# Key pairs laid out by ScalarE, multiplied in two GpSimd instructions and folded from 16 to 8

## The chip, the cores and the metric

One Trainium2 chip, the kernel on one of its cores. The metric is the device time of one execution in microseconds (us). A core has five engines that run their own instruction streams and wait for each other by semaphores: TensorE (PE; its weight loads are PEld), VectorE (DVE), ScalarE (ACT), GpSimd (POOL) and SyncE (SP), which here issues the DMAs.

## What is computed

A model of six stages over 32 images of 256 tokens with 192 features. The change is in the third, an attention with a choice of key pairs, which runs on two halves (t) of 128 tokens of each image, for 12 heads of 16 features. For each token i and head the 8 most similar earlier keys are found; then every set {i, a} (8 of them) and {i, a, b} (28) is scored by the log of the determinant of its Gram matrix, and the output is a mean of the sets' values, weighted by the softmax of the scores:

```python
_, top_idx = jax.lax.top_k(sim, M)                      # M = 8
...
K = k[idx]; V = v[idx]                                  # i, and one or two of the 8
gram = jnp.einsum('cnd,cmd->cnm', K, K)
det = jnp.linalg.det(gram)
log_det = jnp.log(jnp.where(valid, det, 1.0) + 1e-06)
score = SIGN * log_det / float(s + 1) ** ALPHA
dot = jnp.einsum('cnd,d->cn', K, q_i) / HS ** 0.5
w = jax.nn.softmax(dot, axis=1)
out_s = jnp.einsum('cn,cnd->cd', w, V)
...
probs = jax.nn.softmax(scores / TEMP)
y_soft = probs @ outs
```

The off-diagonal Gram entries are 36 dot products of 16 elements for each token and head: 8 of a gathered key with the token's own key, 28 of two gathered keys. The change is in how these 36 are made.

## The kernel before

The attention phase is `dpp_attention_phase`. An image is worked on in 12 steps; a step handles two heads (j = 0, 1) of one half of 128 tokens; steps 0 to 5 are the near half t = 0 (128 keys), steps 6 to 11 the far half t = 1 (256 keys). Every engine runs the same loop of bodies, body i of image n, two images in one turn of a hardware loop, and in body i it does its part of step i and of earlier steps, with fixed lags that the code writes out:

- VectorE, body i: `max` and `max_index` (L2530, L2537) find the 8 best keys of step i; L2545 makes the one-hot matrices of step i-2 (one instruction for a near step, two for a far one, 2048 bf16 elements each); L2554 sums the products of step i-4 into `dots`; then comes one stage of the previous image's scoring (bodies 0, 1, 3 to 7), the value sum `y` (L2513, bodies 8 and 9), or in body 11 the residual (L2520) and the next image's own norms (L2379, L2380).
- ScalarE, body i: casts the found indices of step i (`cast_index`, L2205); copies what TensorE gathered of step i-3, head pair j = 0, out of PSUM (`take_gathered`: keys L2222, values L2223, norms L2224, then `kv_ready`); copies the turned indices (`copy_turned`, L2213) that SyncE then sends out and back as a broadcast; the same for j = 1; then the stage's activation (such as the logarithm of the denominators, L2241), the copies of the next image's projections (L2175 to L2188) and others.
- TensorE, body i: scores of step i+1, the gather of step i-3, j = 0 (L2679; 24 small matmuls in a near step, 48 in a far one), the turn of step i's indices (L2660), the gather of j = 1, then a part of the next image's projections.
- GpSimd, body i: `products` of step i-3, and then in bodies 7 and 8 `weigh` (L2323: values times weights, 1728 elements, one for each half), in body 10 `squares`, in body 11 `split_rest`, in body 0 `split_low`.

So the products of a step that GpSimd makes in body i are summed by VectorE in body i+1. Before the change GpSimd makes them in eight instructions: for each j three over broadcast views of the eight keys (4, 4 and 16 pairs of 16 elements: 64, 64 and 256 elements a partition; L2334), and then for both j together the four remaining pairs (L2339) and the eight with the token's own key (L2340). It can begin on j = 0 while j = 1 is still on its way, and its result has the rows `prod[P, parity, j, 36, 16]`, which L2554 sums over the last axis. The buffers have two parities of step. ScalarE waits for `prod_ready` of two steps earlier before it overwrites `keys`; GpSimd waits for `dots_ready` of two steps earlier before it overwrites `prod`.

Keys, values and products are fp32; the one-hot matrices and the pieces that are gathered with them are bf16.

## Time and profile before

| what | value |
|---|---|
| runs of the kernel before | 6936.29 us (median of 3, 6931.03 to 6949.35) |
| the profiled execution, its own time | 6937.07 us |
| its span on the core | 6935.4 us |
| busy in the span | PE 5118.2, PEld 3716.5, DVE 4327.0, ACT 2100.8, POOL 3276.0 us |
| mean granted TensorE clock | 0.718 |
| `dots` sums (L2554) | 384, 517.0 us, mean 1346 ns |
| products, pairs (L2334) | 2304, mean 514 ns, 1115.6 us |
| products with the own key (L2340) | 384, mean 835 ns, 320.7 us |
| copies of keys (L2222) | 768, mean 264 ns, 202.5 us |

A group's busy time counts each instruction from its start to its end; on ScalarE consecutive instructions overlap, so that the sum of their lengths is more than the time they take. The idle time of an engine is put down to the one whose semaphore came last. The page's chain of the work that ended last covers the end of the last stage of the model only and says nothing of the attention phase, which lies between about 1595 and 4450 us of the span.

### The profile page before, as it was taken

The page shows a single profiled execution, that of the slowest core. Times are in us where ns is not written, and L with a number is a line of the kernel's source. Part 1 is how long each engine was busy: PE and PEld are TensorE (multiplying, and loading weights), DVE is VectorE, ACT ScalarE, POOL GpSimd, SP SyncE. Part 2 cuts the span into 40 slices and gives each one's busy share as a digit, 9 for nine tenths or more (in the row PEclk, how much of TensorE's full clock was granted, in tenths as well). Part 3 has the DMA queues.
Part 4 walks back from the last instruction along what each step waited for, and adds up shares of the span by engine and source line. Part 5 has one row for each costly group of instructions (what it writes and reads, how often), then busy time and mean ns, then how long its engine had stood idle before and what let it go on. Part 6 is the DMA issues. An engine that isn't in the chain of part 4 may idle for free. (4 is left out here: it accounts for less than half of the span.)

```text
span 6935.4 us, 140450 instructions
## 1 busy us (share of the span) xinstructions
PE 5118.2 (74%) x45364; PEld 3716.5 (54%) x45365; DVE 4327.0 (62%) x9002; ACT 2100.8 (30%) x6098; POOL 3276.0 (47%) x4341
## 2 busy tenths in 40 slices
PE   6776766978888888888888888443980997169990
PEld 2333333765555555556555665342860776169990
DVE  5777775227888898898999999722654233212223
ACT  3343333223333333333333333222210332223330
POOL 1222222115666776777776767425236000554447
PEclk8677776996666666666666666556995997579995
DMA  4000000002222222222222222202222002111113
GB/s 138 5 7 5 7 3 6 0 5 71 74 74 70 75 72 72 73 75 71 74 72 72 75 72 75 67 26 73 75 72 68 0 0 60 52 50 46 46 42 109
DMA packets 170739, 369.46 MB, mean 53 GB/s; under 512 B 35650, under 2 KB 100939, under 8 KB 169140
## 3 DMA queue, kind: packets, MB, share of 16 engines
q1 hardware_dynamic: 136404, 283.77, 12.2%
q0 software_dynamic: 33792, 78.69, 3.6%
q8 instruction: 312, 5.11, 0.3%
q14 instruction: 231, 1.89, 0.1%
HBM read 286.86 MB, written 75.50 MB: 52 GB/s over the span
## 5 line engine op out<-in xcount | busy, mean ns | idle before, releaser
L2334 POOL TENSOR_TENSOR l2a_prod<-l2a_keys 128x64 f32<-128x64 f32 (+1 forms) x2304 | 1115.6, 514 | 817.2 <-ACT l2a_norms L2224 808.2
L2679 PE MATMUL l2a_g<-l2a_feat,l2a_onehot 128*128 128x33 bf16 x27648 | 894.1, 187 | 29.9 <-issue 24.8
L2679 PEld LDWEIGHTS l2a_g<-l2a_feat,l2a_onehot 128*128 128x128 bf16 x27648 | 835.8, 103 | 89.5 <-issue 61.1
L2648 PE MATMUL l2a_s<-l2a_qkT 32*128 32x128 f32 (+1 forms) x1536 | 653.6, 518 | 48.3 <-issue 48.3
L1734 POOL TENSOR_TENSOR l_hc<-l_hs,l_bc 128x512 f32<-128x512 f32 x192 | 243.0, 1266 | 803.2 <-DVE l_hs L1808 799.7
L2554 DVE TENSOR_REDUCE l2a_dots<-l2a_prod 128x72 f32<-128x1152 f32 x384 | 517.0, 1346 | 154.3 <-POOL l2a_prod L2340 154.3
L2545 DVE TENSOR_SCALAR l2a_onehot<-l2a_spread,l2a_key_col 128x2048 bf16<-128x2048 bf16 x576 | 544.7, 972 | 52.0 <-PE l2a_g L2679 45.0
L1903 PE MATMUL l_y<-l_hc,l_selT 128*96 128x512 f32 x384 | 316.5, 920 | 287.9 <-POOL l_hc L1734 287.9
L2597 PE MATMUL l2a_a<-l2a_tT,l2a_wqk 96*96 96x256 f32 x1024 | 453.4, 622 | 0.7 <-ACT l2a_tT L2175 0.7
L2648 PEld LDWEIGHTS l2a_s<-l2a_qkT 32*128 32x128 f32 x1536 | 320.5, 259 | 224.6 <-issue 181.7
L440 POOL DMA_INDIRECT rows_in<-l3f_dispatch_xn,l3f_dispatch_at x128 | 122.8, 959 | 651.2 <-ACT l3f_dispatch_xn L416 612.5
L2222 ACT COPY l2a_keys<-l2a_g 128x128 f32<-128x128 f32 x768 | 202.5, 264 | 687.5 <-PE l2a_g L2679 687.1
L652 POOL TENSOR_TENSOR l3f_w_own<-l3f_w,l3f_w_own 96x1536 fp32r<-96x1536 f32 x72 | 252.5, 3507 | 329.7 <-DVE l3f_w_own L753 329.7
L2660 PE MATMUL l2a_t<-l2a_ident_bf,l2a_index 128*16 128x128 bf16 x384 | 101.2, 264 | 368.1 <-ACT l2a_index L2205 367.8
L695 PE MATMUL l3f_expert_h<-l3f_tT,l3f_w_own 96*128 96x256 f32 x2592 | 337.1, 289 | 8.9 <-POOL l3f_w_own L652 6.7
L695 PEld LDWEIGHTS l3f_expert_h<-l3f_tT,l3f_w_own 96*128 96x128 f32 x2592 | 323.8, 193 | 9.6 <-issue 7.1
L2340 POOL TENSOR_TENSOR l2a_prod<-l2a_keys,l2a_feat 128x256 f32<-128x256 f32 x384 | 320.7, 835 | 0.0
L2597 PEld LDWEIGHTS l2a_a<-l2a_tT,l2a_wqk 96*96 96x96 f32 x1024 | 261.9, 270 | 108.0 <-ACT l2a_tT L2175 1.1
L759 DVE TENSOR_TENSOR l3f_tT<-l3f_expert_tp,l3f_tT 96x512 fp32r<-96x512 f32 x72 | 49.5, 687 | 425.3 <-ACT l3f_tT L726 425.3
L735 ACT ACTIVATE l3f_hT<-l3f_expert_h,l3f_b 128x256 f32<-128x256 f32 x432 | 181.0, 470 | 383.6 <-PE l3f_expert_h L695 383.6
L710 PE MATMUL l3f_expert_y<-l3f_w,l3f_hT 128*128 x1728 | 292.6, 326 | 0.0
L1808 DVE TENSOR_TENSOR_SCAN l_hs<-l_dA,l_state,l_dBu 128x512 f32<-128x512 f32 x192 | 262.3, 1366 | 40.0 <-ACT l_dA L1684 33.7
(403 smaller groups left out, 11255.9 us busy)
## 6 DMA issues: line engine op xcount, KB each, us to landing
l2a_spread<-index_rows SPq DMA_DIRECT2D x384, 512.0 KB
rows_in<-main_zeros SPq DMA_DIRECT2D x1, 13824.0 KB, 59.4
l2f_xg<-rows_in SPq DMA_DIRECT2D x72, 192.0 KB, 2.4
rows_out<-l2f_ys POOLq DMA_DIRECT2D x72, 192.0 KB, 2.4
l3f_xg<-rows_in SPq DMA_DIRECT2D x72, 192.0 KB, 2.4
rows_out<-l3f_ys POOLq DMA_DIRECT2D x72, 192.0 KB, 2.4
l3f_w<-in_l3f_w SPq DMA_DIRECT2D x2, 4608.0 KB, 33.6
l_xT<-in_l_xT SPq DMA_DIRECT2D x16, 384.0 KB, 3.9
```

Of the source, the lines that this page charges most:

```text
L652: nc.gpsimd.tensor_tensor(w1_own[:, u, 1, :, :], w1[:, :, bass.ds(e, 1), :].rearrange("p h a f -> p h (a f)"), w1_own[:, u, 0, :, :].bitca ...
L695: ins = nc.tensor.matmul(h_ps[b][:, c % 2, :], w1_own[:, u, wp, h, c * P:(c + 1) * P], tT[:, u, tp_, h, :], start=h == 0 and wp == tp_, st ...
L710: ins = nc.tensor.matmul(y_ps[u][:, t * C:(t + 1) * C], hT[:, u, c, t * P:(t + 1) * P], w2[:, c, bass.ds(e, 1), :].rearrange("p a c -> p ( ...
L1808: nc.vector.tensor_tensor_scan(hs[:, g % 2, :], dA[:, g % 2, :], dBu[:, g % 2, :], state[:, 0, g:g + 1], ALU.mult, ALU.add).then_inc(scan_ ...
L1903: nc.tensor.matmul(y_ps[:, :], selT[:, g, :], hc[:, g % 2, :], start=g == 0, stop=g == G - 1).then_inc(hc_used, 1)
L2334: nc.gpsimd.tensor_tensor(made[:, j, at:at + wide * wide, :].rearrange("p (b a) f -> p b a f", b=wide), key[:, lo:lo + wide, :].unsqueeze( ...
L2340: nc.gpsimd.tensor_tensor(made[:, :, 0:8, :], both, feat[:, u, t, h:h + 4:3, 0:HS].unsqueeze(2).broadcast_to([P, 2, SLOTS, HS]), ALU.mult) ...
L2545: ins = nc.vector.tensor_scalar(onehot[:, s[2] % 2, kt, :, :].rearrange("p k t -> p (k t)"), spread[:, s[2] % 2, :, :].rearrange("p k t -> ...
L2554: nc.vector.tensor_reduce(dots[:, h:h + 4:3, :], prod[:, s[2] % 2, :, :, :], AX.X, ALU.add).then_inc(S["dots_ready"], 1)
L2597: ins = nc.tensor.matmul(o[0:HC, j * T:(j + 1) * T], wqk[:, h, 2 * (k - 1) + j, :], tT[0:HC, h, :], start=h == 0, stop=h == 1)
L2648: nc.tensor.matmul(o, qkT[rows, u, h // 3, t * P:(t + 1) * P], qkT[rows, u, 4 + h // 3, 0:nk], start=True, stop=False, skip_group_check=True)
L2679: ins = nc.tensor.matmul(g_ps[j][:, a * FEAT:(a + 1) * FEAT], onehot[:, s[2] % 2, kt, j * SLOTS + a, :], feat3[:, s[1], kt, piece, h, :], ...
```

## The change

ScalarE now writes the keys of a step not once but as two lists of operands. `left` (36 rows of 16) has the eight keys in rows 0 to 7 and then the 28 first keys of the pairs, `right` (28 rows) the 28 second keys, with the broadcasts done in the copies: seven copies in place of one, 1024 elements in place of 128, for each j, all read from PSUM. GpSimd multiplies `left` by `right` in one instruction for both j (2 x 448 elements), multiplies the first eight rows by the token's own key in a second (256 elements; the same operands as before but in place), waits for its own semaphore `products`, and adds the second eight elements of every row to the first (72 rows, 576 elements). VectorE sums over 8 elements in place of 16. `right` and `left` take the place of `keys` and `prod`. GpSimd waits for both j before it begins, and no longer for `dots_ready`; ScalarE waits for `dots_ready` of two steps earlier in place of `prod_ready`.

```diff
-        keys = m.sb("keys", [P, 2, 2, SLOTS, HS])
+        left = m.sb("left", [P, 2, 2, NCOMB, HS])
+        right = m.sb("right", [P, 2, 2, COMBS, HS])
...
-        prod = m.sb("prod", [P, 2, 2, NCOMB, HS])
...
                     if j == 0:
-                        act.wait_ge(S["prod_ready"], counted(q - 1) if not (isinstance(q, int) and q < 2) else 1)
+                        act.wait_ge(S["dots_ready"], counted(q - 1) if not (isinstance(q, int) and q < 2) else 1)
...
-                    nc.scalar.copy(keys[:, s[2] % 2, j, :, :], src[:, :, 0:HS])
+                    key, lo, hi = src[:, :, 0:HS], left[:, s[2] % 2, j, :, :], right[:, s[2] % 2, j, :, :]
+                    halves = key.rearrange("p (g k) f -> p g k f", g=2)
+                    nc.scalar.copy(lo[:, 0:SLOTS, :], key)
+                    nc.scalar.copy(lo[:, 8:12, :], key[:, 0:8:2, :])
+                    nc.scalar.copy(hi[:, 0:4, :], key[:, 1:8:2, :])
+                    nc.scalar.copy(lo[:, 12:20, :].rearrange("p (g b a) f -> p g b a f", g=2, b=2),
+                                   halves[:, :, 0:2, :].unsqueeze(2).broadcast_to([P, 2, 2, 2, HS]))
+                    nc.scalar.copy(hi[:, 4:12, :].rearrange("p (g b a) f -> p g b a f", g=2, b=2),
+                                   halves[:, :, 2:4, :].unsqueeze(3).broadcast_to([P, 2, 2, 2, HS]))
+                    nc.scalar.copy(lo[:, 20:36, :].rearrange("p (b a) f -> p b a f", b=4),
+                                   key[:, 0:4, :].unsqueeze(1).broadcast_to([P, 4, 4, HS]))
+                    nc.scalar.copy(hi[:, 12:28, :].rearrange("p (b a) f -> p b a f", b=4),
+                                   key[:, 4:8, :].unsqueeze(2).broadcast_to([P, 4, 4, HS]))
...
-                    pool.wait_ge(S["dots_ready"], counted(q - 1) if not (isinstance(q, int) and q < 2) else 1)
-                    made, h = prod[:, s[2] % 2, :, :, :], first_head(s[2])
-                    for j in range(2):
-                        pool.wait_ge(S["kv_ready"], counted(q * 2 + (j + 1)))
...
+                    made, h = left[:, s[2] % 2, :, :, :], first_head(s[2])
+                    pool.wait_ge(S["kv_ready"], counted(q * 2 + 2))
+                    hi = right[:, s[2] % 2, :, :, :]
+                    nc.gpsimd.tensor_tensor(made[:, :, SLOTS:, :].rearrange("p j k f -> p j (k f)"),
+                                            made[:, :, SLOTS:, :].rearrange("p j k f -> p j (k f)"),
+                                            hi.rearrange("p j k f -> p j (k f)"), ALU.mult)
+                    ins = nc.gpsimd.tensor_tensor(
+                        made[:, :, 0:SLOTS, :], made[:, :, 0:SLOTS, :],
+                        feat[:, u, t, h:h + 4:3, 0:HS].unsqueeze(2).broadcast_to([P, 2, SLOTS, HS]), ALU.mult)
+                    ins.then_inc(S["products"], 1)
+                    pool.wait_ge(S["products"], q + 1)
+                    every = made.rearrange("p j k f -> p (j k) f")
+                    nc.gpsimd.tensor_tensor(every[:, :, 0:HS // 2], every[:, :, 0:HS // 2], every[:, :, HS // 2:],
+                                            ALU.add).then_inc(S["prod_ready"], 1)
...
-                        nc.vector.tensor_reduce(dots[:, h:h + 4:3, :], prod[:, s[2] % 2, :, :, :], AX.X, ALU.add
+                        nc.vector.tensor_reduce(dots[:, h:h + 4:3, :], left[:, s[2] % 2, :, :, 0:HS // 2], AX.X, ALU.add
```

ScalarE's order, from the cast of a body's indices to the end of the second take, before:

```order
L2205 CAST l2a_index<-l2a_found 128x16
L2222 COPY l2a_keys<-l2a_g 128x128
L2223 COPY l2a_values<-l2a_g 128x128
L2224 COPY l2a_norms<-l2a_g 128x8
L2213 CAST l2a_indexT<-l2a_t 16x128
L2222 COPY l2a_keys<-l2a_g 128x128
L2223 COPY l2a_values<-l2a_g 128x128
L2224 COPY l2a_norms<-l2a_g 128x8
```

and the same place now, up to the end of the first take and the copy of the turned indices behind it:

```order
L2205 CAST l2a_index<-l2a_found 128x16
L2224 COPY l2a_left<-l2a_g 128x128
L2225 COPY l2a_left<-l2a_g 128x64
L2226 COPY l2a_right<-l2a_g 128x64
L2227 COPY l2a_left<-l2a_g 128x128
L2229 COPY l2a_right<-l2a_g 128x128
L2231 COPY l2a_left<-l2a_g 128x256
L2233 COPY l2a_right<-l2a_g 128x256
L2235 COPY l2a_values<-l2a_g 128x128
L2236 COPY l2a_norms<-l2a_g 128x8
L2213 CAST l2a_indexT<-l2a_t 16x128
```

Each take has nine copies in place of three, and the second take of the body, which is the same nine again, stands behind the first.

GpSimd's order, one body's products, before:

```order
L2334 TENSOR_TENSOR l2a_prod<-l2a_keys 128x64 x2
L2334 TENSOR_TENSOR l2a_prod<-l2a_keys 128x256
L2334 TENSOR_TENSOR l2a_prod<-l2a_keys 128x64 x2
L2334 TENSOR_TENSOR l2a_prod<-l2a_keys 128x256
L2339 TENSOR_TENSOR l2a_prod<-l2a_keys 128x2x64
L2340 TENSOR_TENSOR l2a_prod<-l2a_keys,l2a_feat 128x2x128
```

and now, two bodies in a row:

```order
L2343 TENSOR_TENSOR l2a_left<-l2a_left,l2a_right 128x2x448
L2346 TENSOR_TENSOR l2a_left<-l2a_left,l2a_feat 128x2x128
L2352 TENSOR_TENSOR l2a_left<-l2a_left 128x72x8
L2343 TENSOR_TENSOR l2a_left<-l2a_left,l2a_right 128x2x448
L2346 TENSOR_TENSOR l2a_left<-l2a_left,l2a_feat 128x2x128
L2352 TENSOR_TENSOR l2a_left<-l2a_left 128x72x8
```

Eight instructions are three; all of them stand behind the second take of the body, where three of the eight stood behind the first alone.

## Rows read from the trace of the kernel before

**Rows 1.** The head of the page.

```profile
span 6935.4 us, 140450 instructions
```

**Rows 2.** Busy time of each engine in the attention phase (windows).

```profile
core 0: us, PE busy (x) PEld busy (x) DVE busy (x) ACT busy (x) POOL busy (x), PEclk, DMA share, GB/s
1595.50:4450.00 2854.50, 2375.94 (x32500) 1676.63 (x32500) 2548.30 (x5158) 996.42 (x3979) 1994.79 (x3260) 0.63 0.21 73
```

**Rows 3.** Waits in the attention phase: who waited for whom, us in total, times, longest.

```profile
POOL l2a_prod L2334 <- ACT l2a_norms L2224: 808.2, 333, 4.7
...
DVE l2a_dots L2554 <- POOL l2a_prod L2340: 154.3, 128, 3.2
```

**Rows 4.** Timeline of one image, VectorE: start us, length us.

```profile
2999.79 0.48 DVE L2530 MAX8 l2a_sims<-l2a_s 128x8 f32<-128x128 f32 x2
...
3004.71 1.35 DVE L2554 TENSOR_REDUCE l2a_dots<-l2a_prod 128x72 f32<-128x1152 f32 x1 [1.92 <-POOL l2a_prod L2340]
...
3010.64 1.40 DVE L2545 TENSOR_SCALAR l2a_onehot<-l2a_spread,l2a_key_col 128x2048 bf16<-128x2048 bf16 x2
...
3018.11 1.35 DVE L2554 TENSOR_REDUCE l2a_dots<-l2a_prod 128x72 f32<-128x1152 f32 x1 [0.59 <-POOL l2a_prod L2340]
...
3022.68 1.35 DVE L2554 TENSOR_REDUCE l2a_dots<-l2a_prod 128x72 f32<-128x1152 f32 x1 [1.04 <-POOL l2a_prod L2340]
...
3084.58 1.35 DVE L2554 TENSOR_REDUCE l2a_dots<-l2a_prod 128x72 f32<-128x1152 f32 x1 [0.99 <-POOL l2a_prod L2340]
...
3089.46 0.50 DVE L2530 MAX8 l2a_sims<-l2a_s 128x8 f32<-128x128 f32 x2 [2.14 <-issue]
```

**Rows 5.** Groups of the attention phase by shape, VectorE.

```profile
L2554 DVE TENSOR_REDUCE l2a_dots<-l2a_prod 128x72 f32<-128x1152 f32 x384 | 517.0, 1346 | 154.3 <-POOL l2a_prod L2340 154.3
...
L2464 DVE TENSOR_REDUCE l2a_lane<-l2a_det 128x24 f32<-128x864 f32 x31 | 32.6, 1053 | 1.1
```

**Rows 6.** The same, ScalarE.

```profile
L2222 ACT COPY l2a_keys<-l2a_g 128x128 f32<-128x128 f32 x768 | 202.5, 264 | 687.5 <-PE l2a_g L2679 687.1
...
L2175 ACT COPY l2a_tT<-l2a_a 96x512 f32<-96x512 f32 x31 | 17.5, 563 | 0.4 <-PE l2a_a L2592 0.4
```

**Rows 7.** Timeline of the same image, ScalarE.

```profile
3001.05 0.27 ACT L2222 COPY l2a_keys<-l2a_g 128x128 f32<-128x128 f32 x1 [0.78 <-PE l2a_g L2679]
...
3001.22 0.27 ACT L2223 COPY l2a_values<-l2a_g 128x128 f32<-128x128 f32 x1
...
3015.72 0.92 ACT L2241 ACTIVATE l2a_denom<-l2a_denom 128x864 f32<-128x864 f32 x1 [0.29 <-DVE l2a_denom L2411]
```

**Rows 8.** Groups of the attention phase by shape, GpSimd.

```profile
L2334 POOL TENSOR_TENSOR l2a_prod<-l2a_keys 128x256 f32<-128x256 f32 x768 | 583.2, 759 | 0.0
L2334 POOL TENSOR_TENSOR l2a_prod<-l2a_keys 128x64 f32<-128x64 f32 x1536 | 569.7, 391 | 817.2 <-ACT l2a_norms L2224 808.2
...
L2340 POOL TENSOR_TENSOR l2a_prod<-l2a_keys,l2a_feat 128x256 f32<-128x256 f32 x384 | 320.7, 835 | 0.0
...
L2339 POOL TENSOR_TENSOR l2a_prod<-l2a_keys 128x128 f32<-128x128 f32 x384 | 234.2, 610 | 0.0
...
L2323 POOL TENSOR_TENSOR l2a_values<-l2a_values,l2a_alpha 128x1728 f32<-128x1728 f32 x62 | 194.1, 3130 | 9.5 <-DVE l2a_alpha L2504 9.5
```

**Rows 9.** Timeline of the same image, end of the products and their sum, body 7.

```profile
3051.80 0.65 POOL L2340 TENSOR_TENSOR l2a_prod<-l2a_keys,l2a_feat 128x256 f32<-128x256 f32 x1
...
3053.89 1.34 DVE L2554 TENSOR_REDUCE l2a_dots<-l2a_prod 128x72 f32<-128x1152 f32 x1
```

**Rows 10.** Timeline of the same image, bodies 7 to 9.

```profile
3059.96 3.13 POOL L2323 TENSOR_TENSOR l2a_values<-l2a_values,l2a_alpha 128x1728 f32<-128x1728 f32 x1
...
3060.84 3.53 DVE L2545 TENSOR_SCALAR l2a_onehot<-l2a_spread,l2a_key_col 128x2048 bf16<-128x2048 bf16 x2
...
3065.55 3.10 DVE L2513 TENSOR_REDUCE l2a_y<-l2a_values 128x192 f32<-128x1728 f32 x1
...
3067.54 3.13 POOL L2323 TENSOR_TENSOR l2a_values<-l2a_values,l2a_alpha 128x1728 f32<-128x1728 f32 x1
```

More of the change, by code:

```diff
@@ L2057, in dpp_attention_phase @@
             rest_ready mid_ready split_ready square_ready own_ready scores_ready max_chain found_ready
-            index_ready turned turned_ready rows_out spread_in onehot_ready gathered kv_ready own_values prod_ready dots_ready
+            index_ready turned turned_ready rows_out spread_in onehot_ready gathered kv_ready own_values products prod_ready dots_ready
             diff_ready exp_ready denom_ready lnd_ready gap_ready squared det_ready log_ready shifted probs_ready
@@ L2338, in products @@
-                    both = keys[:, s[2] % 2, :, :, :]
-                    nc.gpsimd.tensor_tensor(made[:, :, 8:12, :], both[:, :, 0:8:2, :], both[:, :, 1:8:2, :], ALU.mult)
-                    nc.gpsimd.tensor_tensor(made[:, :, 0:8, :], both,
-                                            feat[:, u, t, h:h + 4:3, 0:HS].unsqueeze(2).broadcast_to([P, 2, SLOTS, HS]),
-                                            ALU.mult).then_inc(S["prod_ready"], 1)
+                    made, h = left[:, s[2] % 2, :, :, :], first_head(s[2])
```

6 lines of the change are left out of this document (removed).

## Prediction

> **What bounds the kernel now.** I read the page's head first: the span is 6935.4 us [rows 1], against an own time of 6937.07 us of this execution; the median of the runs, 6936.29, is 0.8 us lower. Only the attention phase is touched. Its windows row [rows 2] gives 2854.5 us, in which VectorE is busy for 2548.3 (89%), TensorE for 2375.9, GpSimd for 1994.8 and ScalarE for 996.4. So VectorE is nearest to its limit, and ScalarE has room. Then the waits [rows 3]: GpSimd's products wait for ScalarE's copies in 333 bodies of 384, for 808.2 us, and VectorE's sum of the products waits for GpSimd in 128 of 384, for 154.3 us. The reader is to see a line of hand-overs, TensorE's gather, ScalarE's copies, GpSimd's products, VectorE's sum, in which GpSimd has time to spare on average, but which VectorE waits for in a third of the bodies: four of the twelve of an image. The timeline shows which [rows 4]: body 11 (0.99 us), body 0 (1.92), body 2 (0.59) and body 3 (1.04). The image shown runs from 2999.79 to 3089.46, 89.67 us, 2.14 of them a start of a new turn of the loop that every engine pays. In the other eight bodies the products lie ready. In body 7, one of those with the least room, they end at 3051.80 + 0.65 = 3052.45 and their sum starts at 3053.89: 1.44 us of room [rows 9].
>
> **VectorE's sum: a gain.** 1152 elements take 1346 ns and 864 take 1053 [rows 5], so an element costs 1.02 ns; 576 should take 1053 - 288 x 1.02 = 760 ns. That is 0.59 us less, twelve times an image: 7.0 us. It would all be gain if VectorE never waited longer than now. The bounds are 0.5 us (if the short rows of 8 cost something) and 0.67 (half of 1346).
>
> **ScalarE's copies: later by 1.05 us for each j.** 128 elements take 264 ns and 512 take 563 [rows 6], 0.78 ns an element. A copy of 128 starts 0.17 us before the next one [rows 7], so 0.07 us of that is fixed. Six copies and 896 elements more cost 6 x 0.07 + 896 x 0.78 ns = 1.1 us; I take 1.05, since the start times are rounded to 0.01. At the full length of each copy, fixed part 0.16, it would be 1.66, the upper bound; the elements alone give the lower, 0.7. Over a body that is 2.1 us more on an engine with 65% of its time free, so it does not become the bound. Queued behind the longer takes are the turned indices, whose broadcast is used two bodies later and has a whole body of cover; the projections' copies, for which TensorE has a body's room; and the stage activations. One of these has little room: before the logarithm of the denominators ScalarE waited only 0.29 us [rows 7], so the 1.05 push it, and the next cast of indices behind it, by about 0.75. No DMA is added or moved.
>
> The Trainium skill (ScalarE: Activation LUTs, What ACT_TABLE_LOAD costs) gives such an instruction 186 ns + 0.833 ns an element, with 93 ns of overlap between neighbours. By that the six copies would cost 6 x 0.093 + 0.75 = 1.3 us, and the forecast below would be some 40 us higher; the start-to-start distances of this trace are shorter, and I go by them.
>
> **GpSimd's products: less work, but later.** By the means of the trace a body's eight instructions take 4 x 0.391 + 2 x 0.759 + 0.610 + 0.835 = 4.5 us [rows 8]. For the new ones: 256 elements take 0.65 when nothing is in the way [rows 9], 1728 take 3.13 [rows 8], so 1.69 ns an element and 0.22 fixed. 2 x 448 elements are 1.73 us, the 256 stay at 0.65, the fold of 576 is 1.19, and the wait on its own semaphore some 0.1 (bounds 0 and 0.3): 3.7 us. But the eight could begin when j = 0 was there, and only 2 x 0.391 + 0.759 + 0.610 + 0.835 = 3.0 us stood behind j = 1; now all 3.7 do, and they will be held up now and then as the old ones are (0.835 on average for the 0.65). I take 0.95 us later; the bounds are 0.5 (a slope of 1.45) and 1.6 (a fold that runs at half speed on its runs of 8).
>
> **Together the products come 2.0 us later after the gather of j = 1**, and in bodies 3 to 8, where that gather is so short that the second take stands right behind the first, 2.4. What VectorE pays for it, image by image:
>
> - Bodies 11 and 0: it waits already, and waits longer. TensorE and the projection lie between them and are not all pushed, so 1.2 us each of the 2.0.
> - Body 2: 1.5, since GpSimd was itself a little late there. Body 3: 2.4, with the 0.75 of the late cast. These four are 6.3 us.
> - Bodies 6 and 7: room of 1.44 us, against 2.4 later and a VectorE that comes 0.6 earlier: 1.1 us on average in each, 2.2 together. The gathers there run at TensorE's own pace and do not come earlier.
> - Bodies 8 and 9: GpSimd weighs the values, 3.13 us each [rows 8, 10], behind the products. The trace shows VectorE's one-hots in the way of such an instruction: two of them took 3.53 us beside the weighing that ran from 3059.96 to 3063.09 [rows 10], and take 1.40 alone [rows 4]. The weighing now starts 2 to 3 us later, the value sum (at 3065.55 before, 2.5 us after its weighing ended) must wait for it, and the second weighing follows. I take 2.6 us for both.
> - Bodies 1, 4, 5, 10: nothing; there the sum does not wait for the products now, and they lie ready longer than in body 7.
>
> Sum: 6.3 + 2.2 + 2.6 = 11.1 us lost and 7.0 gained, +4.1 an image. Times 31 (the first and the last image each run half beside nothing) it is +127 us, from 6937.07 to **7064 us**. GpSimd's wait for `dots_ready` goes, and ScalarE's new one on it costs nothing: the sum it waits for stands in VectorE's order before the indices of the same body, which ScalarE has already waited for in its cast.
>
> **Rivals.**
>
> A. *The gain comes through.* VectorE is at 89%, and if the products' delay is taken up by room, the time falls. All of it would be 31 x 7.0 = 217 us, 6720; if only the four bodies that wait keep their waits and gain nothing, 31 x 8 x 0.59 = 146, 6791; with the waits of the sum at half size (5.5 an image), 6937 - 31 x 1.5 = 6891. For it speaks the room in eight bodies; against it that the four waits have none, and that GpSimd now cannot start on j = 0. It decides below a delay of 2.0 x 7.0 / 11.1 = 1.3 us instead of 2.0: both the copies and the GpSimd part would have to be near their lower bounds (0.7 and 0.5).
>
> B. *The long GpSimd instruction holds up VectorE.* The one-hots of 3.53 us [rows 10] show that VectorE can stand still until a GpSimd instruction ends, and then again for the next one. Those of the products were 0.4 to 0.8 us; now there is one of 1.73 and one of 1.19. If two one-hots and two operations of the stages in each image meet them, some 0.9 us each, it is another 3.5 us: 7064 + 31 x 3.5 = 7173 us. The Trainium skill (SBUF — State Buffer, Who interferes with whom) has it as a lock on a shared pair of ports, held for a whole instruction, that also takes in VectorE's operations with two inputs in SBUF, as most of the stages' are; by that rule this would happen in every stage, and the trace agrees for the one-hots.
>
> C. *Gain and loss cancel.* With waits of 7.0 an image, a delay of 1.3 us as above, there is nothing to measure.
>
> D. *The fold does not do what it says*: in runs of 8 elements GpSimd takes as long as for 16, and VectorE's sum no less than 1.1 us. Then half of the gain goes (3.5 an image) and the products come another 0.7 later: about 7064 + 31 x (3 + 3.5) = 7265. I find nothing for it in the rows; it counts with B.
>
> **How the numbers follow.** My forecast, slower by the waits: 0.62. B with D: 0.14. A: 0.17. C: 0.07. The sum is made from one image, and its bounds are wide: with every delay low the image gains 1 us (6906), with every delay high it loses 8 (7185). From C's chance and the low end of the forecast follow the outcomes, where a measurement tells 0.3% (21 us) from no change: faster 0.17, same 0.08, slower 0.75. The range of 6925 to 7190 leaves out most of A and the far end of D, some 0.18 in all.
>
> **What would show it.** The sum at 0.76 us, its waits at 350 to 500 us in place of 154.3, and in six or more bodies of the twelve in place of four. Nine copies in 1.5 us for each take; the three GpSimd instructions at about 1.7 to 2.0, 0.7 and 1.2 us. VectorE busy for about 2550 - 220 us, plus what B adds, in a phase of about 2980; ScalarE near 2300 by the lengths added up (996, and 768 times some 1.7 us). The image at 93 to 94 us. The step that fails first, if I am wrong, is the delay of the products: the distance from the last copy of j = 1 to their end, 3.7 to 4.0 us. If it is right and the kernel is faster, the waits in the four bodies did not grow, which the timeline of one image will show.

## The result, and the profile after

The changed kernel takes 7332.95 us (median of 4 runs, 7331.75 to 7337.76), the kernel before 6937.27 beside it (6931.03 to 6949.35). The ratio is 1.0569, interval 1.0551 to 1.0588: slower by 396 us. The forecast was 7064, with a range up to 7190; the sign was right, the time lies far outside.

The head of the page and the windows row of the attention phase of the changed kernel answer to [rows 1, 2]. The phase is now longer, so the window is 1595.5 to 4900:

```profile
span 7330.4 us, 142755 instructions
...
1595.50:4900.00 3304.50, 2530.64 (x32497) 1769.81 (x32496) 2676.45 (x5198) 1777.73 (x8583) 2107.03 (x1340) 0.55 0.19 64
```

VectorE (the third busy time) has 2676 us where it had 2548, though its sums were cut by 230. ScalarE has 1778 for 996. GpSimd is hardly busier (2107 for 1995, in a longer window), with 1340 instructions for 3260. An image of twelve bodies takes 102.4 us where it took 89.6 (mean of images 2 to 29): +12.8, and 31 x 12.8 = 397 is the whole loss. TensorE's granted clock (the column before the DMA share) is lower, 0.55 for 0.63, but that isn't what makes the keys late: in the same phase ScalarE's copies of the keys waited for TensorE's gathers for 348 us, where they waited for 687 [rows 6]. No run here holds the clock fixed, so a small share of it stays open.

The waits in the attention phase, after, answer to [rows 3]:

```profile
POOL l2a_left L2343 <- ACT l2a_norms L2236: 1061.4, 292, 7.6
...
DVE l2a_dots L2565 <- POOL l2a_left L2352: 488.3, 165, 5.2
```

VectorE's sum waits 334 us longer than before. The timeline of one image of the changed kernel, VectorE, begins body 0 at 3083.40. The sum waits in bodies 0, 1, 3, 7 and 11; this answers to [rows 4]:

```profile
3089.88 0.75 DVE L2565 TENSOR_REDUCE l2a_dots<-l2a_left 128x72 f32<-128x576 f32 x1 [4.05 <-POOL l2a_left L2352]
...
3099.87 0.75 DVE L2565 TENSOR_REDUCE l2a_dots<-l2a_left 128x72 f32<-128x576 f32 x1 [4.09 <-POOL l2a_left L2352]
...
3115.78 0.75 DVE L2565 TENSOR_REDUCE l2a_dots<-l2a_left 128x72 f32<-128x576 f32 x1 [5.24 <-POOL l2a_left L2352]
...
3149.39 0.75 DVE L2565 TENSOR_REDUCE l2a_dots<-l2a_left 128x72 f32<-128x576 f32 x1 [2.02 <-POOL l2a_left L2352]
...
3183.70 0.75 DVE L2565 TENSOR_REDUCE l2a_dots<-l2a_left 128x72 f32<-128x576 f32 x1 [2.05 <-POOL l2a_left L2352]
```

Its groups by shape, after, answer to [rows 5]:

```profile
L2556 DVE TENSOR_SCALAR l2a_onehot<-l2a_spread,l2a_key_col 128x2048 bf16<-128x2048 bf16 x576 | 697.2, 1239 | 11.9 <-DMA l2a_spread<-index_rows 6.8 <-PE l2a_g L2690 5.0
L2565 DVE TENSOR_REDUCE l2a_dots<-l2a_left 128x72 f32<-128x576 f32 x384 | 287.4, 748 | 488.3 <-POOL l2a_left L2352 488.3
...
L2463 DVE TENSOR_TENSOR l2a_det<-l2a_det,l2a_gap 128x672 f32<-128x672 f32 x32 | 81.8, 2557 | 1.1
L2476 DVE TENSOR_TENSOR l2a_det<-l2a_det,l2a_lane 128x864 f32<-128x864 f32 x32 | 81.4, 2544 | 1.1
...
L2475 DVE TENSOR_REDUCE l2a_lane<-l2a_det 128x24 f32<-128x864 f32 x32 | 33.7, 1053 | 1.1
...
L2462 DVE TENSOR_TENSOR l2a_gap<-l2a_gap,l2a_feat 128x672 f32<-128x672 f32 x32 | 27.3, 852 | 0.0
```

The same operations before, in the same view:

```profile
L2545 DVE TENSOR_SCALAR l2a_onehot<-l2a_spread,l2a_key_col 128x2048 bf16<-128x2048 bf16 x576 | 544.7, 972 | 52.0 <-PE l2a_g L2679 45.0 <-DMA l2a_spread<-index_rows 7.0
...
L2465 DVE TENSOR_TENSOR l2a_det<-l2a_det,l2a_lane 128x864 f32<-128x864 f32 x31 | 33.2, 1071 | 1.1
...
L2452 DVE TENSOR_TENSOR l2a_det<-l2a_det,l2a_gap 128x672 f32<-128x672 f32 x31 | 26.6, 858 | 1.1
```

Here is the part that the forecast had left out. Apart from the sum, the change touches none of these operations. The sum of the products is what was forecast (748 ns for 760). But a one-hot takes 1239 ns on average for 972, and `det -= gap` takes 2557 for 858; a reduction of 864 elements, with one input, is unmoved at 1053 [rows 5]. Over all lengths of the phase the one-hots give 153 us more (576 x 0.267) and the other operations of the stages 185: 338 us, 10.9 an image. With the longer waits of the sum (+334), its shorter length (-230), 40 us less of waiting for TensorE before the one-hots, and 15 us more for GpSimd's squares, VectorE's account gives about +417 us, against 395 between the two spans.

Counted over all operations of the phase, VectorE's instructions are longer than the shortest of their own shape by 317 us together before the change and by 638 after. Of the 638, all but 1 us lie in instructions during which a GpSimd instruction was in progress, and the reductions have 0.3 us of it.

The timeline of the same image, GpSimd, shows what ran beside the two:

```profile
3127.54 2.68 POOL L2343 TENSOR_TENSOR l2a_left<-l2a_left,l2a_right 128x896 f32<-128x896 f32 x1 [7.59 <-ACT l2a_norms L2236]
3130.18 1.30 POOL L2346 TENSOR_TENSOR l2a_left<-l2a_left,l2a_feat 128x256 f32<-128x256 f32 x1
3131.56 1.39 POOL L2352 TENSOR_TENSOR l2a_left<-l2a_left 128x576 f32<-128x576 f32 x1
3135.93 2.07 POOL L2343 TENSOR_TENSOR l2a_left<-l2a_left,l2a_right 128x896 f32<-128x896 f32 x1 [2.98 <-ACT l2a_norms L2236]
```

and VectorE in the same stretch:

```profile
3127.43 0.85 DVE L2462 TENSOR_TENSOR l2a_gap<-l2a_gap,l2a_feat 128x672 f32<-128x672 f32 x1
3128.32 2.61 DVE L2463 TENSOR_TENSOR l2a_det<-l2a_det,l2a_gap 128x672 f32<-128x672 f32 x1
...
3136.32 2.60 DVE L2476 TENSOR_TENSOR l2a_det<-l2a_det,l2a_lane 128x864 f32<-128x864 f32 x1
```

Read them together. L2462 has begun when L2343 arrives, so GpSimd's multiplication is the one that grows: 2.68 us for 2.07. L2463 comes next, finds the multiplication in progress and ends 0.71 us after it (3130.93 against 3130.22). Alone it takes 0.86 us, so it stood still for nearly all of the time before. The short product L2346, issued at 3130.18, then takes 1.30 us for its 0.65, since L2463 now has its turn. L2476 starts 0.39 us behind the next multiplication and ends 0.92 us behind its end. Against the means of before (0.86 and 1.07), the two cost VectorE 1.75 and 1.53 us.

The Trainium skill (SBUF — State Buffer, Who interferes with whom) says: "Whoever issues first gets the shared pair for the whole instruction; the other fully blocks", and that an operation of VectorE with two inputs in SBUF meets GpSimd's reads while a reduction never does. These rows agree: the multiplication, issued second, took 2.68 us for 2.07, L2463, issued behind it, 2.61 us for 0.86, and the reduction of 1053 ns is unmoved.

GpSimd's groups, after, answer to [rows 8]:

```profile
L2343 POOL TENSOR_TENSOR l2a_left<-l2a_left,l2a_right 128x896 f32<-128x896 f32 x384 | 858.3, 2235 | 1063.8 <-ACT l2a_norms L2236 1061.4
L2352 POOL TENSOR_TENSOR l2a_left<-l2a_left 128x576 f32<-128x576 f32 x384 | 538.1, 1401 | 30.1
L2346 POOL TENSOR_TENSOR l2a_left<-l2a_left,l2a_feat 128x256 f32<-128x256 f32 x384 | 358.5, 934 | 0.0
```

The 896 elements take 2.07 us with nothing in the way (timeline) and 2235 ns on average, for the forecast's 1.73; the fold takes 1.39 for 1.19. From the last copy of j = 1 to the end of the products it is 4.82 us on average, 3.34 before, and 3.7 to 4.0 in the forecast. ScalarE's timeline answers to [rows 7]; the first and the last of the nine copies of one take:

```profile
3092.16 0.27 ACT L2224 COPY l2a_left<-l2a_g 128x128 f32<-128x128 f32 x1 [4.88 <-PE l2a_g L2690]
...
3093.53 0.27 ACT L2236 COPY l2a_norms<-l2a_g 128x8 f32<-128x8 f32 x1
```

The nine last 1.63 us on average (here 3093.80 - 3092.16) where the three took 0.50: +1.13, for the forecast's +1.05.

### The profile page after: what moved, and what is told of

It reads as the page before. It is cut to its first block and busy times, and to the rows that moved or that the text cites. A ratio compares the mean times of both kernels' runs of the same rounds, so it can differ in the third digit from the quotient of the medians.

```text
span 7330.4 us, 142755 instructions
## 1 busy us (share of the span) xinstructions
PE 5256.5 (72%) x45364; PEld 3799.9 (52%) x45365; DVE 4432.1 (60%) x9002; ACT 2882.5 (39%) x10706; POOL 3387.5 (46%) x2421
## 5 line engine op out<-in xcount | busy, mean ns | idle before, releaser
L2343 POOL TENSOR_TENSOR l2a_left<-l2a_left,l2a_right 128x896 f32<-128x896 f32 x384 | 858.3, 2235 | 1063.8 <-ACT l2a_norms L2236 1061.4
L2659 PE MATMUL l2a_s<-l2a_qkT 32*128 32x128 f32 (+1 forms) x1536 | 710.5, 560 | 46.7 <-issue 46.7
L2556 DVE TENSOR_SCALAR l2a_onehot<-l2a_spread,l2a_key_col 128x2048 bf16<-128x2048 bf16 x576 | 697.2, 1239 | 11.9 <-DMA l2a_spread<-index_rows 6.8
L2565 DVE TENSOR_REDUCE l2a_dots<-l2a_left 128x72 f32<-128x576 f32 x384 | 287.4, 748 | 488.3 <-POOL l2a_left L2352 488.3
L2352 POOL TENSOR_TENSOR l2a_left<-l2a_left 128x576 f32<-128x576 f32 x384 | 538.1, 1401 | 30.1
L2671 PEld LDWEIGHTS l2a_t<-l2a_ident_bf,l2a_index 128*16 128x16 bf16 x384 | 33.5, 87 | 656.5 <-ACT l2a_index L2205 651.8
L2346 POOL TENSOR_TENSOR l2a_left<-l2a_left,l2a_feat 128x256 f32<-128x256 f32 x384 | 358.5, 934 | 0.0
L2224 ACT COPY l2a_left<-l2a_g 128x128 f32<-128x128 f32 x768 | 202.7, 264 | 372.2 <-PE l2a_g L2690 348.2
L2233 ACT COPY l2a_right<-l2a_g 128x256 f32<-128x256 f32 x768 | 332.9, 434 | 0.0
L2231 ACT COPY l2a_left<-l2a_g 128x256 f32<-128x256 f32 x768 | 323.5, 421 | 0.0
```

Of the source, the lines that this page charges most:

```text
L2231: nc.scalar.copy(lo[:, 20:36, :].rearrange("p (b a) f -> p b a f", b=4), key[:, 0:4, :].unsqueeze(1).broadcast_to([P, 4, 4, HS]))
L2233: nc.scalar.copy(hi[:, 12:28, :].rearrange("p (b a) f -> p b a f", b=4), key[:, 4:8, :].unsqueeze(2).broadcast_to([P, 4, 4, HS]))
L2343: nc.gpsimd.tensor_tensor(made[:, :, SLOTS:, :].rearrange("p j k f -> p j (k f)"), made[:, :, SLOTS:, :].rearrange("p j k f -> p j (k f)") ...
L2346: ins = nc.gpsimd.tensor_tensor(made[:, :, 0:SLOTS, :], made[:, :, 0:SLOTS, :], feat[:, u, t, h:h + 4:3, 0:HS].unsqueeze(2).broadcast_to([ ...
L2352: nc.gpsimd.tensor_tensor(every[:, :, 0:HS // 2], every[:, :, 0:HS // 2], every[:, :, HS // 2:], ALU.add).then_inc(S["prod_ready"], 1)
L2556: ins = nc.vector.tensor_scalar(onehot[:, s[2] % 2, kt, :, :].rearrange("p k t -> p (k t)"), spread[:, s[2] % 2, :, :].rearrange("p k t -> ...
```

## The experiments

Each was run beside the kernel before on the same chip; the medians of before were 6931, 6925 and 6923 us in the three sets. "Held up" below is what the lengths of the one-hots and of the stages' other operations, the value sum included, add to before's (560 and 1160 us), each kernel by its own profile. In the first set the change is taken apart.

### copies_only: ScalarE's copies alone

```diff
-                    nc.scalar.copy(keys[:, s[2] % 2, j, :, :], src[:, :, 0:HS])
+                    key, lo, hi = src[:, :, 0:HS], spare_low[:, j, :, :], spare[:, j, :, :]
+                    nc.scalar.copy(keys[:, s[2] % 2, j, :, :], key)
+                    nc.scalar.copy(lo[:, 0:4, :], key[:, 0:8:2, :])
...
```

The six further copies go to buffers that nothing reads; the products are as before.

> The kernel before, with ScalarE's six additional copies of each take written into spare buffers that nobody reads; GpSimd and VectorE as before. It prices ScalarE's part alone. Theory A (late products): the products come 1.1 to 1.5 us later, the waits of the sum grow from 154 to 300-400 us, the kernel takes 7040 to 7120 us. Theory B (the long GpSimd instructions hold up VectorE): little of the 396 us comes from here, under 7010 us; VectorE's busy time within 25 us of the 4327.0 of before, since no GpSimd instruction is longer.

Measured: 7044.55 us, ratio 1.0176 (1.0152 to 1.0199), +113. The sum waits 286.4 us, 132 more. One-hots take 929 ns (25 us less in all), the stages 1166 us: VectorE is held up no more than before. So the copies cost only waits, 3.6 us an image in time (113 / 31). The time lies in theory A's range and above theory B's, the waits just below A's.

### both_first: GpSimd begins when j = 1 is there

```diff
-                        pool.wait_ge(S["kv_ready"], counted(q * 2 + (j + 1)))
+                        pool.wait_ge(S["kv_ready"], counted(q * 2 + 2))
```

> The kernel before, where GpSimd waits for the keys of both j before its first product. It prices the lost early start alone. Theory A: the products end up to 1.2 us later, waits of the sum 200 to 300 us, 6970 to 7030 us. Theory B: within 0.5% of before (under 6970), VectorE's busy time unchanged.

Measured: 6965.42, ratio 1.0054 (1.0035 to 1.0072), +34; the sum waits 261.4. The products end 4.63 us after the last copy, almost as late as in the changed kernel (4.82). This lateness of +1.3 us behind j = 1 cost 34 us. It isn't the price of lateness by itself: the sum waits 107 us more, but with the same instructions only moved in time, VectorE is also held up for some 47 us less (one-hots 9, stages 38). How much the two engines collide depends on when they meet, and every run below moves that a little.

### fold_only: the fold behind the old products

```diff
-                                            ALU.mult).then_inc(S["prod_ready"], 1)
+                                            ALU.mult).then_inc(S["products"], 1)
+                    pool.wait_ge(S["products"], q + 1)
+                    every = made.rearrange("p j k f -> p (j k) f")
+                    nc.gpsimd.tensor_tensor(every[:, :, 0:HS // 2], every[:, :, 0:HS // 2], every[:, :, HS // 2:],
+                                            ALU.add).then_inc(S["prod_ready"], 1)
...
-                        nc.vector.tensor_reduce(dots[:, h:h + 4:3, :], prod[:, s[2] % 2, :, :, :], AX.X, ALU.add
+                        nc.vector.tensor_reduce(dots[:, h:h + 4:3, :], prod[:, s[2] % 2, :, :, 0:HS // 2], AX.X, ALU.add
```

> The kernel before with only the fold on GpSimd and the shorter sum on VectorE; copies and the eight product instructions as before. The sum saves 230 us of VectorE's busy time; the products end 1.5 us later. Theory A: about 7 waiting places x 1.5 us against 7.2 us saved, so 6960 to 7060 us. Theory B: the fold of 1.4 us holds up VectorE as well: its one-hots and stage operations gain 80 us or more of busy time over before (after the 230 are taken off), and the kernel takes 7060 or more.

Measured: 7185.32 (7179.76 to 7206.97), ratio 1.0367 (1.0347 to 1.0386), +254. Two rows of its profile, VectorE's groups of the attention phase:

```profile
L2549 DVE TENSOR_SCALAR l2a_onehot<-l2a_spread,l2a_key_col 128x2048 bf16<-128x2048 bf16 x576 | 680.3, 1208 | 28.1 <-PE l2a_g L2683 19.2 <-DMA l2a_spread<-index_rows 8.2
...
L2558 DVE TENSOR_REDUCE l2a_dots<-l2a_prod 128x72 f32<-128x576 f32 x384 | 286.6, 746 | 376.8 <-POOL l2a_prod L2345 376.8
```

The sum saves 230 us and waits 223 more, so these two cancel; the loss is the 292 us for which VectorE is held up (one-hots +136, stages +156). Of the three parts tried alone, the fold of 1.4 us costs most.

### no_fold: copies and two products, no fold

```diff
+                    made, h = left[:, s[2] % 2, :, :, :], first_head(s[2])
+                    pool.wait_ge(S["kv_ready"], counted(q * 2 + 2))
+                    hi = right[:, s[2] % 2, :, :, :]
+                    nc.gpsimd.tensor_tensor(made[:, :, SLOTS:, :].rearrange("p j k f -> p j (k f)"),
+                                            made[:, :, SLOTS:, :].rearrange("p j k f -> p j (k f)"),
+                                            hi.rearrange("p j k f -> p j (k f)"), ALU.mult)
...
+                    ins.then_inc(S["prod_ready"], 1)
...
+                        nc.vector.tensor_reduce(dots[:, h:h + 4:3, :], left[:, s[2] % 2, :, :, :], AX.X, ALU.add
```

> The changed kernel without the fold: GpSimd's two multiplications, VectorE sums all 16 elements. The products end 1.5 us earlier, the sum takes 0.6 us more. Theory A: the waits of the sum fall from 488 to under 300 us, and the time to 7150-7230 us. Theory B: the multiplication of 896 elements (2.24 us on average) still holds up VectorE, so the lengthened one-hots and stage operations keep two thirds or more of their 335 us, and the time stays above 7200 us.

Measured: 7172.26, ratio 1.0355 (1.0335 to 1.0375), +241; waits 270.4, one-hots 995 ns (+13 us in all), stages +165. The sum's waits, and one of the stages' operations, 1071 ns before:

```profile
DVE l2a_dots L2561 <- POOL l2a_left L2346: 270.4, 122, 4.2
```

```profile
L2472 DVE TENSOR_TENSOR l2a_det<-l2a_det,l2a_lane 128x864 f32<-128x864 f32 x32 | 77.6, 2424 | 1.1
```

Both numbers that theory B gave were missed: the 178 us are a little over half of what the change holds up, not two thirds, and the time is under 7200. A's range for the time held, but A has no place for the 178 us. Note that here GpSimd works less than before (one product of 2.13 us for seven of 4 x 0.39 + 2 x 0.76 + 0.61 = 3.7) and still VectorE's stages lose 165 us. It isn't the amount of GpSimd's work alone.

Taken alone, the copies cost 113 us, the later start 34 and the fold 254. Their sum of 401 is near the whole, 396, by coincidence. It leaves out the merging of the products into large instructions, and the parts change each other's price: the copies and the two merged products together cost 241, where copies and later start alone make 147, and the fold costs 155 on top of them (396 - 241) for 254 alone. The path that does add up is copies 113, then late start with the products merged 128, then the fold 155. In the middle step the sum even waits 16 us less than with the copies alone (270.4 for 286.4), so its 128 us are not of late products: one-hots and stages are 199 us longer than with the copies alone, and some smaller waits are shorter.

### idle_fold: the same fold, off the path

The next question is what the fold costs where nobody waits for it. Before's products are announced first, and the fold's result goes to a buffer that nothing reads.

```diff
                                             ALU.mult).then_inc(S["prod_ready"], 1)
+                    pool.wait_ge(S["prod_ready"], counted(q + 1))
+                    every = made.rearrange("p j k f -> p (j k) f")
+                    nc.gpsimd.tensor_tensor(spare[:, :, :], every[:, :, 0:HS // 2], every[:, :, HS // 2:], ALU.add)
```

> The kernel before, with the same fold of 576 elements on GpSimd, but after the products are announced and into a spare buffer that nobody reads. No product is later, except where GpSimd had no time to spare. Theory A (only late products cost): within 0.5% of before, 6915-6965 us. Theory B (a GpSimd instruction in progress holds up VectorE's one-hots and its operations on two SBUF operands): one-hots and stages together gain 100-290 us of busy time and the kernel takes 7030 to 7200 us.

Measured: 7233.21, ratio 1.0443 (1.0425 to 1.0462), +309. The waits, and the one-hots:

```profile
DVE l2a_dots L2558 <- POOL l2a_prod L2341: 191.0, 115, 3.7
```

```profile
L2549 DVE TENSOR_SCALAR l2a_onehot<-l2a_spread,l2a_key_col 128x2048 bf16<-128x2048 bf16 x576 | 638.8, 1136 | 33.4 <-PE l2a_g L2683 25.7 <-DMA l2a_spread<-index_rows 7.4
```

The sum waits 37 us more, and VectorE is held up for 94 + 151 = 245. This is the clearest of the runs: 1.4 us of GpSimd work a body that no one waits for, on an engine with 860 us idle in the phase, costs 0.8 us a body (309 / 384). The time is even above the 7200 that theory B gave as its upper end. The run isn't quite clean: the next products end 0.7 us later behind the last copy (4.03 for 3.34), and it is the 245 us held up that make most of the 309. Against it, fold_only's 254 shows what shortening the sum gives net of the later products and of a little more holding up: 309 - 254 = 55 us, where rival A had 217.

### idle_fold_pieces: that fold in six

```diff
-                    nc.gpsimd.tensor_tensor(spare[:, :, :], every[:, :, 0:HS // 2], every[:, :, HS // 2:], ALU.add)
+                    for r in range(0, 2 * NCOMB, 12):
+                        nc.gpsimd.tensor_tensor(spare[:, r:r + 12, :], every[:, r:r + 12, 0:HS // 2],
+                                                every[:, r:r + 12, HS // 2:], ALU.add)
```

> The same idle fold in six instructions of 96 elements, some 0.4 us each: 2.4 us of GpSimd time in place of 1.4. Theory A: no less time than the run with one idle fold. Theory B, with the length of the instruction deciding: VectorE is held up for less each time but can be more often; the added time is half or less of that of the run with one. If instead any GpSimd work costs VectorE its time, it adds more than that run.

Measured: 7236.02, ratio 1.0446 (1.0427 to 1.0465): no difference from idle_fold, so the half or less of theory B was missed, and so was the rise expected if any GpSimd work costs the same. But it is not the same loss. The one-hots fall to 928 ns, less than before's 972, and the stages to +111, so VectorE is held up for 86 us in place of 245. In exchange a piece of 96 elements takes 453 ns, six of them 2.7 us for 1.45, and GpSimd, busy for 2977 of 3304 us, is now late itself:

```profile
DVE l2a_dots L2560 <- POOL l2a_prod L2341: 254.7, 141, 4.4
DVE l2a_y L2519 <- POOL l2a_values L2324: 101.4, 41, 3.3
...
DVE l2a_feat L2385 <- POOL l2a_square L2305: 59.6, 31, 2.5
```

The six short instructions hold VectorE up for about a third of what the long one did, in more GpSimd time; cutting is paid for on GpSimd. Since the products also move in time here, it isn't shown that the length alone makes the difference (see per_j).

### pieces: the changed kernel, multiplication in four and fold in three

```diff
+                    for r in range(0, COMBS, 7):
+                        low = made[:, :, SLOTS + r:SLOTS + r + 7, :].rearrange("p j k f -> p j (k f)")
+                        nc.gpsimd.tensor_tensor(low, low, hi[:, :, r:r + 7, :].rearrange("p j k f -> p j (k f)"),
+                                                ALU.mult)
...
+                    for r in range(0, 2 * NCOMB, 24):
+                        row = every[:, r:r + 24, :]
+                        ins = nc.gpsimd.tensor_tensor(row[:, :, 0:HS // 2], row[:, :, 0:HS // 2],
+                                                      row[:, :, HS // 2:], ALU.add)
```

> The changed kernel with the multiplication of the pairs in four instructions (224 elements each) and the fold in three (192 elements each): some 1 us more work for GpSimd a body. Theory A: the products come 1 us later, so slower than the changed kernel's 7333, 7400-7500 us. Theory B: one-hots and stages lose at least 100 us of the 335 us by which they grew; the time is 7250 to 7350 us.

Measured: 7350.39, ratio 1.0618 (1.0598 to 1.0638), a little worse than the change. VectorE is held up for 141 us in place of 338, as theory B had it; the products come 6.02 us after the last copy, and the sum waits 655.2. One loss is traded for the other.

### weigh_pieces: the weighing of the values in four

The kernel before, but its longest GpSimd instruction [rows 10] cut into four of 432 elements.

```diff
-                    held = values[:, u, t, :, :, :]
-                    nc.gpsimd.tensor_tensor(held, held, alpha[:, t * HEADS:(t + 1) * HEADS, :].unsqueeze(3).broadcast_to(
-                        [P, HEADS, SLOTS + 1, HS]), ALU.mult).then_inc(S["pv_ready"], 1)
+                    for a in range(0, HEADS, 3):
+                        held = values[:, u, t, a:a + 3, :, :]
+                        ins = nc.gpsimd.tensor_tensor(held, held, alpha[:, t * HEADS + a:t * HEADS + a + 3, :].unsqueeze(
+                            3).broadcast_to([P, 3, SLOTS + 1, HS]), ALU.mult)
+                    ins.then_inc(S["pv_ready"], 1)
```

> The kernel before with GpSimd's weighing of the values (3.13 us, twice an image) in four instructions of 432 elements (about 0.95 us). Theory A: GpSimd has 0.7 us more to do twice an image, with room: no change (6915-6950). Theory B: the two one-hots of body 8, 3.61 us together instead of 1.46, wait for at most one or two pieces: 1 to 1.5 us less an image, and some of it again in body 9: 6870 to 6910 us, faster than before.

Measured: 6895.34 (6880.72 to 6903.29), ratio 0.9958 (0.9942 to 0.9973): faster than before by 0.4%, a small gain, but its interval does not reach 1. The timeline of one image, GpSimd and VectorE:

```profile
3025.72 4.46 POOL L2324 TENSOR_TENSOR l2a_values<-l2a_values,l2a_alpha 128x432 f32<-128x432 f32 x4 [1.40 <-DVE l2a_alpha L2506]
...
3027.03 2.37 DVE L2547 TENSOR_SCALAR l2a_onehot<-l2a_spread,l2a_key_col 128x2048 bf16<-128x2048 bf16 x2
3029.32 1.34 DVE L2556 TENSOR_REDUCE l2a_dots<-l2a_prod 128x72 f32<-128x1152 f32 x1
```

The two one-hots take 2.37 us where they took 3.53 [rows 10], the weighing 4.46 where it took 3.13; its user is far enough off. An image takes 87.9 us for 89.6. In all, the one-hots are shorter by 14 us, the stages are unchanged, the sum waits 21 us less for the products and the one-hots 15 us less for TensorE: the shorter one-hots of body 8 are the smaller part of the gain in VectorE's account, and what made the waits shorter wasn't tried.

### idle_memset: work that only writes

After the announced products a tiny addition and a memset of 1536 elements, 1.37 us.

```diff
+                    pool.wait_ge(S["prod_ready"], counted(q + 1))
+                    nc.gpsimd.tensor_tensor(small[:, :], made[:, 0, 0, :], made[:, 1, 0, :], ALU.add)
+                    nc.gpsimd.memset(spare[:, :], 1.0)
```

> The kernel before, with GpSimd writing 1536 constants into a spare buffer after each announcement of the products (and a sum of 16 elements ahead of it). It keeps GpSimd busy for about as long as the idle fold did, but reads nothing. If what holds VectorE up is that both read through one port: the stages (operations on two SBUF operands) keep within 50 us of before's 1160 us of busy time, while the one-hots (a fast mode that writes by both ports) may grow; time under 7050. If any GpSimd instruction holds VectorE up: stages +100 us or more and 7150 to 7250 us as with the idle fold. If only late products cost (theory A): within 0.5% of before.

Measured: 7161.14, ratio 1.0339 (1.0322 to 1.0357), +238. One-hots 1169 ns (+113 us), stages +66, waits +22. The result lies between the two expectations: the time is that of "any GpSimd instruction", the stages gain more than 50 us but less than 100. So a GpSimd instruction without a read holds up the one-hots as the fold does (1136 ns), and the two-input operations less. In its timeline, GpSimd and VectorE, an operation of the stages runs beside the memset in 0.34 us, the shortest that this shape takes here, and the next four, beside an instruction that reads, take 2.43 for the 1.0 that they need alone:

```profile
3004.60 1.37 POOL L2347 MEMSET l2a_spare<- 128x1536 f32 x1
3005.93 1.71 POOL L2312 TENSOR_TENSOR l2a_rest_f<-l2a_feat 128x792 f32<-128x792 f32 x1
...
3005.76 0.34 DVE L2401 TENSOR_TENSOR l2a_top<-l2a_sims,l2a_own 128x192 f32<-128x192 f32 x1
3006.14 2.43 DVE L2403 TENSOR_TENSOR l2a_ex<-l2a_sims,l2a_top 128x96 f32<-128x96 f32 x4
```

Part of the +66 may come from the tiny addition and from products that moved; that is argued, not shown.

### per_j: the multiplication split by j

```diff
+                    for j in range(2):
+                        pool.wait_ge(S["kv_ready"], counted(q * 2 + (j + 1)))
+                        low = made[:, j, SLOTS:, :].rearrange("p k f -> p (k f)")
+                        nc.gpsimd.tensor_tensor(low, low, right[:, s[2] % 2, j, :, :].rearrange("p k f -> p (k f)"),
+                                                ALU.mult)
```

> The changed kernel with the pairs' multiplication split by j (448 elements, some 1.1 us each), the first of them as soon as the keys of j = 0 are there. Theory A and B both: the products end about 1 us earlier and the longest instruction is half as long; the waits of the sum fall to about 400 us, one-hots and stages lose 50 to 100 us: 7180 to 7280 us in place of 7333. If splitting costs GpSimd more than the early start gives, as in the run in pieces: 7330 or more.

Measured: 7250.63, ratio 1.0472 (1.0457 to 1.0488), +328: 68 us less loss than the change. The waits fall to 334.4. The time is as expected, but not the holding up, which I had expected to fall by 50 to 100 us: it grows (one-hots 1264 ns, stages +226, 394 us together for the change's 338). Two instructions of 1.1 us block at least as much as one of 2.1. The gain is the waits' 154, less the 56 that are held up more and some smaller waits.

### short_all: all long instructions of before cut

The weighing in six, and the two subtractions of 792 elements in four each.

```diff
-                    nc.gpsimd.tensor_tensor(rest_f[:, :, :, :], feat[:, u, :, :, :], feat3[:, u, :, 0, :, :],
-                                            ALU.subtract).then_inc(S["rest_ready"], 1)
+                    for a in range(0, HEADS, 3):
+                        ins = nc.gpsimd.tensor_tensor(rest_f[:, :, a:a + 3, :], feat[:, u, :, a:a + 3, :],
+                                                      feat3[:, u, :, 0, a:a + 3, :], ALU.subtract)
+                    ins.then_inc(S["rest_ready"], 1)
...
```

> The kernel before with every long GpSimd instruction cut: the weighing in six (288 elements, about 0.65 us), the two halves of the bf16 split in four each (198 elements). If the length of an instruction in progress is what VectorE pays: another 10 to 25 us less than with the weighing in four (6895), 6865 to 6890. If GpSimd's added fixed times (0.2 us each, 16 an image) delay the products instead: 6900 to 6930.

Measured: 6932.59 (12 runs, 6915.80 to 6946.76), ratio 1.0014 (1.0004 to 1.0024): my expectation missed, the gain of weigh_pieces is gone. The one-hots stay at 947 ns, but the six pieces of the weighing now end behind their user:

```profile
L2328 POOL TENSOR_TENSOR l2a_values<-l2a_values,l2a_alpha 128x288 f32<-128x288 f32 x384 | 296.1, 803 | 28.3 <-DVE l2a_alpha L2510 28.3
```

They take 6 x 0.80 = 4.8 us in place of 3.1, and the value sum waits for them for 33.9 us, for 3.3 before and 8 in weigh_pieces. Which of the two cuts cost the rest was not tried.

## Why the prediction was wrong

**Right.** The sum: 748 ns for 760, 7.4 us an image for the forecast's 7.0. The copies: +1.13 us for +1.05. That the loss outweighs the gain, and that VectorE stays the engine that sets the time. The waits as a total, 334 / 31 = 10.8 us an image for the forecast's 11.1, agree by luck, as shown below.

**The step that failed** is rival B, in its price and in its place. I priced the held-up VectorE at 3.5 us an image, two one-hots and two operations of the stages at 0.9 each, gave it with D a chance of 0.14, and left it out of the forecast. The runs show 10.9 us an image, 338 us in all: a term as large as all the longer waits. idle_fold, where hardly anything but this can cost time, shows that it is real: +309 us. With it the forecast's own sum would have been 11.1 + 10.9 - 7.0 = 15.0 an image against the measured 12.8; VectorE's waits for other engines were a little shorter (the one-hots' for TensorE 5.0 us for 45.0). The rows for it were at hand: two one-hots at 3.53 us for 1.40 [rows 4, 10], and before's means above their shortest, as products of 835 ns for 0.65 [rows 8, 9], showed that it already happened in every image; before's trace has 317 us of it in all. I let it count only where a long instruction was new, and by a count of four meetings that no row gave. idle_fold gives what I should have had: 0.8 us a body for 1.4 us of GpSimd work that falls beside VectorE's one-hots and two-input work. By that measure alone the fold was a loss, since it buys 0.6 us on VectorE for 0.8. It isn't a fixed rate: no_fold has less GpSimd work than before and still holds VectorE up for 178 us.

**The second step** is GpSimd's own time. I took 1.69 ns an element from the weighing, 1728 elements in 3.13 us [rows 8], where one of the operands is one value repeated over a row. With two full operands it is 2.07 us for 896, 2.3 ns an element, and 1.39 for 576, 2.4. That the repeated operand makes the difference is argued; no run changes it alone. The means of the pairs' own products, 391 ns for 64 elements and 759 for 256 [rows 8], have a slope of 1.92 ns and were the nearer rows. The products end 1.48 us later behind the last copy and the copies 1.13 later behind the gather, together 2.6 in place of the forecast's 2.0 to 2.4.

The Trainium skill (GPSIMD Engine Reference, 3.1 Elementwise — side-by-side cycle accounting) gives 4497 ns for a tensor_tensor of 2048 elements; an estimate from that is 2.2 ns each and 1.97 us for the multiplication. The trace's 2.07 us is near that, and not near my 1.73.

**By bodies** the waits fell otherwise than forecast, and the total is right by luck: a longer delay (2.6 us) met fewer places that wait (five bodies in the image shown, not six or more). By the forecast's own proportion 2.6 would have given some 14 us an image. In the image of [rows 4] the sum waited in bodies 11, 0, 2 and 3; in every second image it also waited in body 1, which the one image by hand did not show. Means over both kinds, after less before: body 11 +1.5 (forecast 1.2), body 0 +1.4 (1.2), body 1 +1.1 (0), body 2 +0.4 (1.5), body 3 +3.6 (2.4), body 7 +2.0 (1.1), and none in 6, 8 and 9, for which I had 3.7. ScalarE's new wait on `dots_ready`, put at nothing, shows up in 5 bodies for 19.8 us in all. That VectorE, itself held up, comes later there than the products, and so doesn't wait, fits the timelines above; no run takes the holding up away and leaves the lateness, so it is argued.

**The other rivals.** A is out: in the pair fold_only and idle_fold 55 us were left of its 217. C is out. D is out: the fold of 576 takes 2.4 ns an element, as the multiplication does, and the sum is short.

## What to carry to other kernels

Before moving work from VectorE to GpSimd, look in the trace for how much of VectorE's remaining work can be held up by it (here the operations with two inputs in SBUF, and the one-hots, 2048 bf16 elements in 0.74 us), and put a price on every microsecond of GpSimd work there, also where nobody waits for the result: here 0.8 us a body for 1.4. Small operations count too: in the changed kernel a tensor_scalar of 24 fp32 elements, with one input, takes 1221 ns on average for 180. A mean above the shortest instance of the same shape, in the rows of either engine, is the sign that they already meet. Cutting the longest GpSimd instruction where its user is far off, as in weigh_pieces, gave 0.4% here, and cutting further, as in short_all, lost it again. Cutting what someone waits for gained nothing (pieces), except where the first piece could start earlier (per_j), and then by the earlier start.

## What the hardware showed that I had not expected

- Idle time of GpSimd is not free time: idle_fold added 1.45 us of unused work a body to an engine with 860 us idle, and the kernel lost 309 us.
- A GpSimd instruction that only writes (a memset of 1.37 us) held up one-hots as one that reads (1169 against 1136 ns, 972 before).
- GpSimd's tensor_tensor of the same type costs differently by shape: the weighing, where one operand is repeated, takes 0.91 us for 432 elements (the shortest in weigh_pieces) and 3.12 for 1728, 1.7 ns for each element more; with two full operands it is 0.37 us for 96 (idle_fold_pieces) and 2.07 for 896, 2.1 ns for each more.
- Fewer and larger instructions were worse: no_fold has two product instructions a body for eight, 3.0 us of them for 4.5, and the stages' operations took 165 us more.
